# Weight, mask and table preparation as a lane of the first order table, loads in six groups

## The reference

```
xn = layernorm(x)
s  = gated recurrence(xn)          # W1: 128 -> 3*256, a scan over the tokens, W2: 256 -> 128
g  = silu(two layers of: local attention (8 heads of 64, window 64, rotary tables),
          then a gated MLP (128 -> 2*341 -> 128))
x  = x + s * g
xn = layernorm(x)
s  = 16-head attention over 512 tokens (q, k of 16, v of 64 per head), output projection
g  = silu(experts or a bias)
x  = x + s * g
```

## Time and profile before

| what | us |
|---|---|
| median of three runs | 3555.42 (3549.72 to 3556.77) |
| the profiled execution | 3553.1 |
| span in its trace | 3551.3 |
| PE busy | 3004.4 (85%) |
| ACT busy | 2564.8 (72%) |
| DVE busy | 2481.0 (70%) |
| POOL busy | 900.7 (25%) |

### The profile page before, as it was taken

The page is one execution under the profiler, slowest core; times in us unless marked ns, Lnnn a source line. Parts: engine busy times, 40 slices in busy tenths (PEclk is TensorE's granted clock), DMA queues, the critical chain, the costliest instruction groups (busy, mean ns, idle before and its releaser), DMA issues.

```text
span 3551.3 us, 54939 instructions
## 1 busy us (share of the span) xinstructions
PE 3004.4 (85%) x20144; PEld 1444.1 (41%) x20144; DVE 2481.0 (70%) x4573; ACT 2564.8 (72%) x5722; POOL 900.7 (25%) x685
## 2 busy tenths in 40 slices
PE   4667898988989798998989898898979889897787
PEld 2333343534444353444434343444435344443243
DVE  2465877868587786858688686868778686866524
ACT  2455787868787786868778686877778687876655
POOL 1131322313132231313232231313233131323100
PEclk7889999999999999999999999999999999998999
DMA  2001001010101101010100101010010101010210
GB/s 77 1 1 45 22 19 55 15 60 17 58 14 41 33 15 60 19 55 19 53 22 15 59 14 55 19 56 18 28 47 15 60 19 53 19 53 10 68 54 21
DMA packets 113449, 122.78 MB, mean 35 GB/s; under 512 B 13427, under 2 KB 86685, under 8 KB 113181
## 3 DMA queue, kind: packets, MB, share of 16 engines
q1 hardware_dynamic: 113180, 119.26, 10.5%
HBM read 64.70 MB, written 54.53 MB: 34 GB/s over the span
## 4 chain that ended last, share of the span: by engine, by line
PE 51%; DVE 22%; ACT 18%; issue 5%; POOL 3%; SPq 1%; DMA 0%; ACTq 0%; DVEq 0%; POOLq 0%
PE pb L611 21%; PE o_bank L611 12%; PE s L611 7%; PE e L611 6%; DVE nmax L1340 5%; ACT ex L1063 3%; PE e L704 3%; DVE stat L1266 2%; PE pb L732 2%; DVE side L1202 2%; DVE scratch L1278 1%; POOL scratch L1443 1%; ACT mlp_h L1020 1%; ACT scratch L996 1%; DVE stat L1237 1%
## 5 line engine op out<-in xcount | busy, mean ns | idle before, releaser
L1340 DVE TENSOR_REDUCE nmax<-s 128x1 f32<-128x512 f32 x1024 | 689.4, 684 | 339.6 <-PE s L611 331.4
L1063 ACT ACTIVATE ex<-s,nmax 128x512 f32<-128x512 f32 x1024 | 700.3, 686 | 188.1 <-DVE nmax L1340 176.0
L611 PE MATMUL o_bank<-ex,vsc 128*64 128x512 f32 x2048 | 514.7, 630 | 14.4 <-POOL vsc L1477 12.2
L611 PE MATMUL s<-qs,ks 96*128 96x512 bf16 x1024 | 390.0, 405 | 148.2 <-ACT ex L1063 137.5
L611 PE MATMUL e<-wqkv,hsh 128*128 128x512 f32 x768 | 457.6, 680 | 51.2 <-ACT scratch L963 31.6
L1477 POOL TENSOR_TENSOR vsc<-vrow,rinv 128x256 f32<-128x256 f32 x256 | 163.6, 639 | 1133.8 <-DVE rinv L1351 1128.7
L1438 POOL TENSOR_TENSOR scratch<-scratch 128x1024 f32<-128x1024 f32 x128 | 301.3, 2354 | 586.5 <-DVE scratch L1247 418.7
L1443 POOL TENSOR_TENSOR scratch<-scratch,stat 128x1024 f32<-128x1024 f32 x128 | 243.9, 1905 | 403.9 <-DVE stat L1259 403.9
L996 ACT ACTIVATE scratch<-pb,stat 128x128 f32<-128x128 f32 x1024 | 292.5, 376 | 56.0 <-DVE stat L1266 56.0
L611 PEld LDWEIGHTS s<-qs,ks 96*128 96x128 bf16 x1024 | 98.7, 99 | 456.5 <-ACT ex L1063 294.4
L611 PE MATMUL pb<-vb,scratch 128*64 128x65 f32 (+1 forms) x2176 | 193.1, 233 | 93.0 <-DVE scratch L1278 58.7
(11 more groups left out here) (196 smaller groups left out, 5707.6 us busy)
## 6 DMA issues: line engine op xcount, KB each, us to landing
parts_store<-side SPq DMA_DIRECT2D x64, 384.0 KB, 2.6
qs<-parts_store SPq DMA_DIRECT2D x128, 192.0 KB, 2.7
ks<-parts_store SPq DMA_DIRECT2D x128, 192.0 KB, 3.2
parts_store<-side SPq DMA_DIRECT2D x64, 256.0 KB, 2.9
parts_store<-side SPq DMA_DIRECT2D x64, 128.0 KB, 2.7
xin<-in_L_attn_x SPq DMA_DIRECT2D x16, 256.0 KB, 3.6
out<-o1T SPq DMA_DIRECT2D x16, 256.0 KB, 3.9
wqkv<-in_L_ffn_wqkv SPq DMA_DIRECT2D x1, 1536.0 KB
```

The costliest lines, as they stand in the source:

```text
L611: return pe.matmul(o, l, r, start=start, stop=stop, skip_group_check=True)
L1063: A(ex[:, w % 2, j, :], s_bank[c % 2][:], ACT.Exp, bias=nmax[:, c % 8:c % 8 + 1], accum_out=rsum[:, w % 2, j:j + 1]).then_inc(GA, 1)
L1340: V.tensor_reduce(nmax[:, c % 8:c % 8 + 1], s_bank[c % 2][:], X, ALU.max, negate=True).then_inc(GV, 1)
```

## The change

The preparation becomes a flow `setup` with eleven steps on a lane `w` of the first phase. Its PE steps write the banks `s0` and `s1` in place of `pb` and `o_bank`. The raw masks and tables are loaded into `vrow` in place of `scratch`. SP issues `const`, then the tokens of sequence 0, then the loads in the order first layer's qkv weight (`wqkv`), `tables`, `network`, `gru`, `global`, each group with its own semaphore. Each step waits for the groups it uses; the first users of a prepared tile get a `need()` on the step that makes it. The tables for `first` are new on PE, ACT and DVE; those for `middle` and `last` and POOL's are as before.

```diff
+def setup_steps():
+    return [("masks",), ("tab", 0), ("qk",), ("bias", 0), ("bias", 1), ("gates",), ("tab", 1), ("v", 0), ("v", 1), ("o", 0), ("o", 1)]
...
+    if phase == "first":
+        out["w"] = [("setup", 0, s) for s in STEPS["setup"]]
...
-        "pe": ("4s11pqpqprp2qprpq2rq2pq3rqrpqpq2rq3rqs12rps2ps3p2s3pq2p2qspr2pq2psrsqprpr2qr2pqpqrpqp2rsrpqpqrp3r3p2"
...
+        "pe": ("3s2w3p2wps5pq2pqwrpq2pqprprqrpqpqwrqwrqprqprq2rq2rq13rs3ps3psps2pspqps2qpr2pqr2pqpspqrsqrq3r3pr2pqpqr"
...
-        raw_masks = sc(0, 2 * P)
+        raw_masks = vrow[:, 0, 0:2 * P]
...
+            ("wqkv", wqkv[:, 0, :], a["L0_ffn_wqkv"][0]),
+            ("tables", raw_masks, a["const"][:, 3 * P:5 * P]),
...
+            ("network", wqkv[:, 1, :], a["L0_ffn_wqkv"][1]),
+            ("gru", gru_w1[:], a["L0_attn_W1"]),
...
+            ("global", raw_o, a["L1_attn_output_proj"].rearrange("d h v -> d (h v)")),
...
-            for dst, src in LOADS:
-                sp.dma_start(dst, src).then_inc(loaded, 16)
+            sp.dma_start(const[:], a["const"][:, 0:3 * P]).then_inc(loaded["const"], 16)
...
             load_x(0)
+            for group, dst, src in LOADS:
+                sp.dma_start(dst, src).then_inc(loaded[group], 16)
...
-            pe.wait_ge(loaded, N_LOADS)
...
-            pe.wait_ge(prep_dve, 2)
-            pe.wait_ge(prep_act, 1)
-            pe.wait_ge(prep_pool, 1)
+            pe.wait_ge(cleared, 1)
+            pe.wait_ge(loaded["const"], LOADED["const"])
+
+            def setup_does(b, s):
+                kind, SE = s[0], setup.sem["pe"]
+                if kind == "qk":
+                    pe.wait_ge(loaded["global"], LOADED["global"])
+                    for r in range(2):
+                        pe.transpose(s_bank[0][:, P * r:P * r + P], raw_q[:, r, :], ident)
+                        last = pe.transpose(s_bank[0][:, P * (2 + r):P * (2 + r) + P], raw_k[:, r, :], ident)
+                elif kind == "bias":
+                    l = s[1]
+                    if l:
+                        need(pe, setup, "dve", b, ("bias", 0), "b")
+                    else:
+                        pe.wait_ge(loaded["network"], LOADED["network"])
...
+                        if l == b == 0:
+                            pe.wait_ge(loaded["wqkv"], LOADED["wqkv"])
...
+                if kind == "gates":
+                    need(act, setup, "dve", b, s, "n")
...
+                elif kind == "tab":
+                    l = s[1]
+                    dve.wait_ge(loaded["tables"], LOADED["tables"])
```

More of the change, by code:

```diff
@@ L235 @@
 KEEP_MARKS = {"x0": {"pool": ["c"]}, "x1": {"pool": ["c"]}}
+SETUP_MARKS = {
+    "masks": {"dve": ["m"]},
+    "tab": {"dve": ["t"]},
+    "qk": {"pe": ["t"], "dve": ["c"]},
+    "bias": {"pe": ["b"], "dve": ["b"]},
+    "gates": {"dve": ["n", "d", "g"], "act": ["e", "l", "f"]},
+    "v": {"pe": ["t"], "act": ["c"]},
+    "o": {"pe": ["t"], "act": ["c"]},
+}
 STEPS = {
+    "setup": setup_steps(),
     "pre": [("x",), *norm_steps("in")],
@@ L376, in build @@
         attn, post = (flows["attn0"], flows["attn1"]), (flows["post0"], flows["post1"])
-        loaded, routing_loaded = sem("weights_loaded"), sem("routing_loaded")
+        loaded = {n: sem(f"{n}_loaded") for n in ("const", "wqkv", "tables", "network", "gru", "global")}
+        routing_loaded = sem("routing_loaded")
         x_loaded, out_stored = sem("x_loaded"), sem("out_stored")
@@ L486, in build @@
         LOADS = [
[L487 to L503, removed]
+            ("wqkv", wqkv[:, 0, :], a["L0_ffn_wqkv"][0]),
+            ("tables", raw_masks, a["const"][:, 3 * P:5 * P]),
+            ("tables", base_tab.rearrange("p c t k d -> p (c t k d)"), a["const"][:, 5 * P:]),
         ]
@@ L716, in attn_does @@
                     need(pe, qkv[l], "act", b, ("tk", t), "t")
+                    if l == b == t == 0:
+                        need(pe, setup, "dve", 0, ("masks",), "m")
                     for par in range(2):
@@ L790, in post_does @@
                         need(pe, f, *(("dve", b, ("a", j - 1), "a") if j else ("act", b, ("g", JM - 1), "g")))
+                    if kind == "g" and b == j == 0:
+                        need(pe, setup, "dve", 0, ("bias", l), "b")
                     at = HID * (kind == "g") + P * j
@@ L815, in glob_does @@
                         need(pe, post[1], "dve", b, ("normed", "out"), "n")
+                    if b == 0 and n < 2:
+                        need(pe, setup, "act", 0, ("o", 1), "c")
                     mm(s_bank[n % 2][:], xn1[:, P * (n // 2):P * (n // 2) + P], wv1[:, 512 * (n % 2):512 * (n % 2) + 512])\
@@ L1052, in glob_does @@
                         need(act, mix, "pool", b - 1, ("scale_v", H1 - 1), "v")
+                        if b == 0:
+                            need(act, setup, "dve", 0, ("tab", 1), "t")
                     A(vrow[:, n // 2, 512 * (n % 2):512 * (n % 2) + 512], s_bank[n % 2][:], ACT.Copy).then_inc(GA, 1)
@@ L1207, in gru_does @@
                 elif kind == "g5":
+                    if b == 0:
+                        need(dve, setup, "dve", 0, ("gates",), "g")
                     need(dve, gru, "act", b, ("g4", j), "g")
@@ L1235, in qkv_does @@
                     t = s[1]
+                    if b == t == 0:
+                        need(dve, setup, "dve", 0, ("tab", l), "t")
                     need(dve, f, "act", b, ("k", t), "sq")
```

202 lines of the change are left out of this document (128 added, 74 removed).

## The result

The change makes the kernel faster, and by far more than forecast: 3510.15 us against 3555.07 measured beside it (medians of four runs each), a ratio of 0.9878, 95% interval 0.9861 to 0.9895. The forecast was 3538 with a range from 3524 to 3552; the time lies outside it, on the fast side.

What follows compares the result with a forecast made beforehand. No engine is busy throughout; order and waits in the first two turns decide. Earlier start 21.1, less 4.5 (turn 0's tiles) and 1.0 (preparation), plus 1.5 (turn 1): 17.1 us less, 3538 us, range 3524 to 3552.

Steps and rivals of the forecast that it cites:

- Carried as a shift: Turns 2 to 17, tables unchanged: gains or losses of the first two turns reach the end as a plain shift.
- a sign of being wrong: Wrong if PE's load wait ends after 31, clock stays 0.50 beyond 70 us, or later stretch changes over 3 us.
- The load gate: Start: qkv0 still waits for the last load, landing at 26.1; first product at 29.6 for 50.7, lead 21.1 us.
- I take the stall as gone: Start, SP's load issues: the 4.1 us stall at `output_proj` vanishes, so SP ends at 22.6.
- Tile 1's delay: Turn 0: bias columns, preparation and sequence 1's tokens ahead make tile 1's q copy 3.4 us late.
- I take 1.0 off: Turn 0, tile 2: k and v follow the score at the higher clock; 1.0 us back, leaving 4.5 lost.
- cost of the preparation: Turn 0: remaining preparation (`gates`, `tab` 1, `v` 1, both `o`) costs 1.0 us, near nothing since PE idles a third.
- The other moves of turn 1: Turn 1, moves besides the priced one: both signs, given no term and left to the range.
- The priced move: Turn 1: sequence 1's norm goes behind the copy of v on DVE; gain 1.5 us, 1.0 to 2.4.
- The stall that stays: Rival, start: SP's queue fills again, `global` lands at 30.2, lead 4.1 us smaller; 3542 us, chance 0.15.
- No change: Rival, turns 0 and 1: all 11.2 us of preparation return on the chain, 5.5 lost in two tiles; 3551, chance 0.11.
- the third: Rival, slower: new order keeps PE's clock at 0.50 from 85 to 130 us; 3565 us, chance 0.08.

Runs made afterwards that it cites:

- e1: Kernel before the change with the changed order of turns 0 and 1 on TensorE, ScalarE and VectorE, old loads and preparation in front; 3529.5 us, ratio 0.9937.
- after: The changed kernel as a whole, against the kernel before the change; 3510.15 us, ratio 0.9878.
- e8: Changed kernel with the steps that wait for the last load groups moved behind the query product of sequence 0's tile 2; 3495.98 us, ratio 0.9839 to before.
- e2: Changed kernel's loads, front and preparation lane, with the old order of the other steps in turns 0 and 1; 3536.57 us, ratio 0.9959 to before.
- e4: Kernel before the change with the new order only up to turn 0's last step, without the preparation lane; 3543.48 us, ratio 0.9977.
- e7: Kernel before the change with only sequence 1's first layernorm moved behind sequence 0's first value and rotary steps; 3555.53 us, ratio 1.0008.
- e3: Kernel before the change with the new order only behind turn 0's last step (turn 1); 3535.1 us, ratio 0.9953.
- e6: Kernel before the change with turn 1 in the new order only up to the beginning of sequence 1's first layer; 3545.38 us, ratio 0.9981.
- e10: Kernel before the change with turn 1 in the new order only from the beginning of sequence 1's first layer on; 3547.18 us, ratio 0.9967.
- e9: Kernel before the change with turn 1's first softmax steps and their copies moved ahead of the gate steps; 3569.74 us, ratio 1.0038.

## Why the prediction was wrong

The gain was 44.7 us in the trace, where 17.1 were forecast. Of the 27.6 us between them turn 1 has 19.2, turn 0 9.6 and the rest 3.3, while the start gave 4.5 less than forecast.

**Carried as a shift: right in the main.** What the first two turns gain reaches the end. With the new order turn 1 has the same length in three kernels that begin it 39 us apart (e1, after, e8), and e8's earlier start reaches the first maximum one to one. With the old order it does not hold so plainly: e2 begins turn 1 17.3 us earlier than before and needs 5.3 more for it, e4 begins 6.4 earlier and needs 4.9 less. In e2 it is TensorE's busy time (6.5 us more), in e4 that (2.9 less) and the idle time (2.0 less). The argument that no step waits for a clock time left out that TensorE's own clock can come out otherwise. The rest changed by 3.3, just over the 3 that the prediction had set as a sign of being wrong; the experiments spread over 7.0 there.

**The load gate: right mechanism, mis-sized.** "I take the stall as gone" failed: small loads behind large ones now carry it, and the wait ended after 31, which the prediction had named as a sign of being wrong. The term was 26.1 and measured 31.1; the lead was 21.1 and measured 16.6. The mistake was to take the landing of one load in a quiet queue for one that ends a run of large loads, and its upper bound of 30.2 allowed for the stall, not for the landing as well. What stands behind the gate was sized well: 3.05 us to the first product, forecast 3.55.

**Turn 0: wrong sign.** Tile 1's delay is there, but 2.0 us (ScalarE's copy of q is 14.15 behind the first product, 12.15 before), where 3.4 was forecast, and the next product wins half of it back. ScalarE's copy:

```profile
48.29 0.58 ACT L1028 ACTIVATE scratch<-e 128x512 f32<-128x512 f32 x1
```

k and v of tile 1, and k and v of tile 2, on TensorE now:

```profile
48.91 1.12 PE L640 MATMUL e<-wqkv,hsh 128*128 128x512 f32 x2 [1.61 <-ACT scratch L1028]
50.73 2.00 PE L640 MATMUL e<-wqkv,hsh 128*128 128x512 f32 x2 [0.69 <-ACT scratch L1028]
...
64.50 1.12 PE L640 MATMUL e<-wqkv,hsh 128*128 128x512 f32 x2
66.31 1.13 PE L640 MATMUL e<-wqkv,hsh 128*128 128x512 f32 x2 [0.69 <-ACT scratch L1028]
```

And before, k of tile 1 and v of tile 2:

```profile
63.52 2.07 PE L611 MATMUL e<-wqkv,hsh 128*128 128x512 f32 x2 [2.35 <-ACT scratch L963]
...
80.94 2.07 PE L611 MATMUL e<-wqkv,hsh 128*128 128x512 f32 x2 [0.69 <-ACT scratch L963]
```

k of tile 1 runs at the high clock of 2.4 GHz (1.12 us; at the low one 2.07), behind bias columns and transposes that kept TensorE at work. "I take 1.0 off" for the clock was too little: k and v of tile 2 run at 1.12 and 1.13 where 2.07 stood, so that pair and k of tile 1 alone have 2.8 us. By the end of tile 2's v the chain is 1.0 us behind the old one, where 4.5 was forecast. From there to the 4.1 us gained at the end of the turn are 5.1 more; they come behind tile 2, where the prediction counted the new order as nothing. The transposes of tile 3's q, before and then now:

```profile
111.72 1.05 PE L704 MATMUL e<-const,scratch 128*128 128x128 f32 x4
```

```profile
91.04 0.63 PE L754 MATMUL e<-const,scratch 128*128 128x128 f32 x4 [0.79 <-POOL scratch L1526]
```

They begin 61.0 us behind the first product before and 56.9 now, and there the 4.1 us are complete. In the old order tile 1's `oturn` and `wo` stood ahead of them, in the new order they stand behind. How much of the 5.1 us is this move and how much the clock was not separated. No cost of the preparation shows in the chain (e2), as its reason said.

**Turn 1: the step that failed.** "The other moves of turn 1 have both signs and stay in the range" took them at nothing and left them to a range with 1.0 to 2.4 us for this turn; the turn gained 20.7. The priced move was worth nothing by itself (e7), the unpriced ones nearly everything (e1, e3, e6, e10). What they do is not a removal of one wait, but less waiting in both halves of the turn: TensorE idles 18.3 us less with the same work. The idle 60 us of the turn, which stand in the trace of before, were the bound on the fast side that the prediction didn't work out.

**The rivals.** The stall that stays has its mechanism seen, in another shape. No change and slower did not come; but the mechanism of the third, an order under which TensorE's clock stays low, is real: e9, 13 us slower, shows it in turn 1 (17.0 us more busy time). The Trainium skill, "TensorE: Matmul & The Clock Gate", Part 1, says that waits for data throttle the clock; e9 agrees (5.37 us of idle time, in which the granted clock falls from 0.94 to 0.50, then 2.07 in place of 1.13).

What stays open: which moves in each half of turn 1 carry the gain together. Only three were tried alone. Why the granted clock of one and the same table differs from kernel to kernel is open too.

## What to carry to other kernels

A changed order is to be priced by the idle time of the stretch that it reorders, not by the few moves that one can follow: read how much the bounding engine idles there, and let the range reach for a good part of it (here 18 of 60 us). A single wait is not worth its length while the steps that were pushed back stand ahead of the next thing needed (5.67 us became 1.05, and the next 1.72 became 4.29). When two traces are compared, set busy and idle time of the bounding engine apart: here the idle time told the orders apart, while the busy time for the same instructions ran from 136 to 156 us with the granted clock. And where an in-order engine waits for the last of a list of loads, ask first whether the step that needs it must stand first: moving it and a few steps with it gave 14 us more.

## What was not expected

- The granted clock of the profile says nothing at the start of some traces. In e8 it stands at 1.00 over 17.9 to 44.2 us, in which a pair of products takes 2.08 as at the granted 0.50 in before. The Trainium skill, "TensorE: Matmul & The Clock Gate", Part 1, warns that the recorded events of the gate can't be fully trusted; these rows agree. Durations of one repeated product are the safer reading. The windows of e8:

```profile
17.90:44.20 26.30, 17.12 (x26) 5.99 (x27) 12.70 (x33) 9.63 (x17) 6.59 (x3) 1.00 0.44 121
```

- The same table of turn 0 gave 97.0 and 103.2 us (e4, e1), by TensorE's busy time alone (64.2 and 70.8; idle 32.8 and 32.5).
- The 1 KB loads `ln_g`, `ln_b` and `b` took 1.90, 1.13 and 0.99 us to issue behind a large one. Before, the same three took 0.43, 0.47 and 0.47.
